# Strassen-form layer 1 of an MLP kernel: the seven products of a round issued in another order, the helper engines' lists reordered with them

## Chip, cores, metric

One NeuronCore of a Trainium2 chip. The metric is device time in microseconds (us) of one launch. PE is the matmul engine (TensorE), DVE is VectorE, ACT is ScalarE, SP issues the large transfers.

## What is computed

Eight sequences of 256 tokens with 512 features go through an attention block, two gelu MLPs of hidden width 2048, and a small per-sequence expert block with a layer norm. Cut to what matters:

```python
attn_out = softmax((x @ Wq) @ (x @ Wk).T * scale) @ (x @ Wv) @ Wp + bp
cms_out  = gelu(attn_out @ cW1 + cb1) @ cW2 + cb2 + one_hot(codes)
modifier = gelu(concat([attn_out, cms_out]) @ mW1 + mb1) @ mW2 + mb2
x = clip(x + cms_out + modifier, 0, 1)
h = gelu(x @ W_down[e] + b_down[e]) @ W_up[e] + b_up[e]      # e per sequence
out = layernorm(x + h) * ln_w[e] + ln_b[e]
```

## The kernel before

**Split numbers.** Every fp32 operand is kept as a high and a low part (`..._hi` written by ACT, `..._lo` = value minus high part by DVE), and every matmul is three matmuls: low weight by high data, high by high, high by low (`mm3`, lines 214 to 216 of the profile).

**Batches and rounds.** The work runs in two batches of four sequences. In each, `pe_mlp` goes through 26 rounds, `it` = 0 to 25. Chunk `i` of the hidden width (24 chunks of 256: 0 to 7 of the first MLP, 8 to 15 the attention half of the second MLP's input, 16 to 23 its other half) starts in round `it = i` and ends in round `i + 1`. Chunks 0 to 7 and 16 to 23 also have a second layer, eight short steps L0 to L7 in round `i + 2`; chunks 8 to 15 are parked and added in later. So rounds 2 to 9 and 18 to 25 hold layer-2 steps between the products, and rounds 10 to 17 hold none.

**The seven products.** Layer 1 of a chunk is a 2 by 2 block product in Strassen's form: seven products, P1 to P7, six matmuls each. P1, P2, P5, P6 of chunk `it` and P7, P4, P3 of chunk `it - 1` share a round. They accumulate in three PSUM banks: P1, P6, P7, P4 one after another on one bank, P2 on the second, P5 and P3 on the third. Between two products on a bank, ACT or DVE takes the running sum:

- s1 after P1 (P6 waits for it), s2 after P6 (P7 waits), c22 after P7 (P4 waits), c21 after P4 (P1 of chunk `i + 2` waits);
- c11 after P2 (P2 of `i + 2` waits); s5 after P5 (P3 and c22 need it), c12 after P3 (P5 of `i + 2` waits).

c11, c22 and c12 are DVE additions at line 975. s1, s2, s5 and c21 are ACT copies (line 555) for chunks below 16; from chunk 16 on they are DVE additions, lines 955 and 965. The gelu of a sum is ACT's line 631.

**What sets the order.** Nothing is scheduled: each engine runs its own hand-written list, and semaphores tie the lists together. The lists of the MLP are `pe_mlp`, `act_mlp` and `dve_mlp`. A waiting instruction holds all that stands behind it on its engine. In a round DVE does, in this order: low parts of the late weights of chunk `it` (two `w_lo` at line 901), four weight sums of chunk `it + 1` (`s_f`, lines 915 to 920), c11 and c22, low parts of the first weights of `it + 1` (three `w_lo`), then c12, with additions of layer 2 (line 1005), low parts of the hidden values (`hid_lo`) and of the second weight (`w_lo`, 128x1024) between them. In rounds 10 to 14 the inputs of the last eight chunks are made (`t_f` at line 1029, `tc_hi` on ACT, `tc_lo` on DVE), ahead of c12, and in rounds 14 and 15 a 128x2048 addition (line 1048) stands behind c12.

Of the kernel before, what the change touches and what calls it, by code (L numbers as in the profile page):

```python
# [17 lines left out]
def build(nc, x, codes, experts, Wq, Wk, Wv, Wp, bp, cW1, cb1, cW2, cb2, mW1, mb1, mW2, mb2,  # L18
# [43 lines left out]
    with ExitStack() as ctx:  # L62
# [376 lines left out]
        def pe_mlp(pe, b):  # L439

            def l1(i, bank, w, t, start):
                hi, lo = (tc_hi, tc_lo) if phase_of(i) == 2 else (ta_hi, ta_lo)
                which = phase_of(i) // 2
                if i in (0, 1, 2 * NQ, 2 * NQ + 1):
                    pe.wait_ge(t_lo, 14 * b + 7 * which + T_NO[t] + 1)
                for k in range(2):
                    last = mm3(ps[BANKS[i % 2][bank]][:, :], w1_hi[i % 2][:, W_NO[w], k, :],
                               w1_lo[i % 2][:, W_NO[w], k, :], hi[:, T_NO[t], k, :], lo[:, T_NO[t], k, :],
                               start and k == 0, k == 1, skip_group_check=True)
                return last  # L450

            def first(i, which):
                g = quad(b, i)
                if which == 1:
                    pe.wait_ge(w1_l1, 3 * g + 2)
                    if i >= 2:
                        pe.wait_ge(c21_done, g - 1)
                    elif b and i == 0:
                        pe.wait_ge(z_sum, 4 * b + 1)
                    else:  # L460
                        pe.wait_ge(ao_done[0], 2 * b + 1 + i)
                    l1(i, 0, "A11", "B11", True).then_inc(p1_mm, 1)
                elif which == 2:
                    if i >= 2:
                        pe.wait_ge(c11_done, g - 1)
                    elif b and i == 0:
                        pe.wait_ge(z_sum, 4 * b + 2)
                    else:
                        pe.wait_ge(ao_done[1], 2 * b + 1 + i)
                    l1(i, 1, "A12", "B21", True).then_inc(p2_mm, 1)  # L470
                elif which == 5:
                    pe.wait_ge(w1_l1, 3 * g + 3)
                    if i >= 2:
                        pe.wait_ge(c12_done, g - 1)
                    else:
                        pe.wait_ge(ao_done[3 - i], 2 * b + 2)
                    l1(i, 2, "S1", "T1", True).then_inc(p5_mm, 1)
                else:
                    pe.wait_ge(s1_done, g + 1)
                    l1(i, 0, "S2", "T2", False).then_inc(p6_mm, 1)  # L480

            def second(i, which):
                g = quad(b, i)
                if which == 7:
                    pe.wait_ge(w1_l2, 2 * g + 2)
                    pe.wait_ge(s2_done, g + 1)
                    l1(i, 0, "S3", "T3", False).then_inc(p7_mm, 1)
                elif which == 4:
                    pe.wait_ge(c22_done, g + 1)
                    l1(i, 0, "A22", "T4", False).then_inc(p4_mm, 1)  # L490
                else:
                    pe.wait_ge(s5_done, g + 1)
                    l1(i, 2, "S4", "B22", False).then_inc(p3_mm, 1)

            def l2(i, k):
                r = l2_of(b, i)
                reg, slot = phase_of(i) // 2, r % 2
                t, j = divmod(k, KT)
                if k == 0:
                    pe.wait_ge(w2_l, r + 1)  # L500
                    pe.wait_ge(hid_l["11"], r + 1)
                    pe.wait_ge(hid_l["21"], r + 1)
                elif k == KT:
                    pe.wait_ge(hid_l["12"], r + 1)
                    pe.wait_ge(hid_l["22"], r + 1)
                if 8 * (r - RB * b) + k >= 2:
                    pe.wait_ge(evac, 8 * r + k - 1)
                elif b:
                    pe.wait_ge(z_sum, 4 * b + 3 + k)
                else:  # L510
                    pe.wait_ge(ao_done[2 + k], 1)
                for c in range(2):
                    w = slice(j * P, (j + 1) * P)
                    last = mm3(ps[6 + k % 2][:, :], w2_hi[reg][:, slot, c, w], w2_lo[reg][:, slot, c, w],
                               hid_hi[reg][:, slot, c, t, :], hid_lo[reg][:, slot, c, t, :], c == 0, c == 1)
                last.then_inc(l2_mm, 1)

            for which in (1, 2):
                first(0, which)
            for which in (1, 2):  # L520
                first(1, which)
            for which in (5, 6):
                first(0, which)
            second(0, 7)
            for which in (5, 6):
                first(1, which)
            for which in (4, 3):
                second(0, which)
            for it in range(2, QB + 2):
                new, old, dn = it < QB, it - 1 < QB, has_l2(it - 2)  # L530
                for step, which in enumerate((1, 2, 7, 5, 6, 4, 3)):
                    if which in (1, 2, 5, 6):
                        if new:
                            first(it, which)
# [26 lines left out]
        def act_w1_first(act, b, i, part):  # L561
            g = quad(b, i)
            a11, a12, _, _ = raw_blocks(i)
            if part == 0:
                act.wait_ge(w1_in[i % 2], 16 * (g // 2) + 16)
                if i >= 2:
                    act.wait_ge(p6_mm, g - 1)
                else:
                    for e in range(KT):
                        act.wait_ge(pv_mm[e], 2 * b + 1 + i)  # L570
                act_copy(w1_hi[i % 2][:, 0, :, :], a11).then_inc(w1_h1, 1)
                act_copy(w1_hi[i % 2][:, 1, :, :], a12).then_inc(w1_h1, 1)
# [201 lines left out]
        def act_mlp(act, b, tail):  # L774
            cms_t = {10: ("B11", "B21"), 11: ("T1",), 12: ("T2", "T3"), 13: ("B22",), 14: ("T4",)}
            for it in range(QB + 2):
# [9 lines left out]
                    act_s(act, b, 1, 1)  # L786
                if 0 < it < QB - 1:
                    act_w1_first(act, b, it + 1, 0)
                if new and ph != 1 and it != 1:
                    act_gelu(act, b, it, "11")  # L790
                if it == 0:
                    act_gelu(act, b, 1, "11")
                if 0 < it < QB - 1:
                    act_w1_first(act, b, it + 1, 1)
                if old and pph != 1:
                    act_gelu(act, b, it - 1, "22")
                    act_hid(act, b, it - 1, "22")
                if it and new and ph < 2:
                    act_s(act, b, it, 5)
                if old and pph != 1:  # L800
                    act_w2(act, b, it - 1)
                if it and new and ph < 2:
                    act_s(act, b, it, 2)
                if old:
                    if pph == 1:
                        act_c21_copy(act, b, it - 1)
                    else:
                        act_gelu(act, b, it - 1, "21")
                        act_hid(act, b, it - 1, "21")
                for name in cms_t.get(it, ()):  # L810
                    act_t(act, b, 1, name)
                if it == QB and not tail:
# [426 lines left out]
        def dve_mlp(dve, b):  # L1239
            for it in range(QB + 2):  # L1240
# [18 lines left out]
                if it == 0:  # L1259
                    dve_c(dve, b, 0, "11")  # L1260
                    dve_c(dve, b, 1, "11")
                elif new and it > 1:
                    dve_c(dve, b, it, "11")
                late = pph == 1
                if 0 < it < QB - 1 and not late:
                    dve_w1_first(dve, b, it + 1)
                down(1)
                if old:
                    dve_c(dve, b, it - 1, "22")
                if 0 < it < QB - 1 and late:  # L1270
                    dve_w1_first(dve, b, it + 1)
                if old and pph != 1:
                    dve_hid(dve, b, it - 1, "11")
                down(2)
                if new and ph == 2:
                    dve_s_pre(dve, b, it, 5)
                if old and pph != 1:
                    dve_hid(dve, b, it - 1, "22")
                down(3)
                if old and pph != 1:  # L1280
                    dve_w2(dve, b, it - 1)
                if new and ph == 2:
# [281 lines left out]
```

## Time and profile before

| what | value |
|---|---|
| median of 3 runs | 1131.21 us (1131.04, 1131.21, 1133.42) |
| profiled execution, its own time | 1133.84 us |
| its span, first to last instruction | 1132.1 us |
| mean granted TensorE clock | 0.977 |
| PE busy | 1064.7 us (94%) |
| DVE busy | 810.8 us (72%) |
| ACT busy | 501.3 us (44%) |
| PE waits for DVE or ACT inside the MLP rounds | 35.3 us |

The profiled execution's own time is 1.7 us above its span. PE's busy time counts the pipelined ends of matmuls, so a product is best read by the distance between starts. Rounds are found in the timeline by the names: `ta` is the input of chunks 0 to 15, `tc` of chunks 16 to 23, and PE's wait before a product is in brackets behind its first matmul. In this execution round 11 of the first batch starts at 313.60 us, round 15 at 353.46, round 17 at 375.14, round 18 at 388.22; the second batch runs the same rounds 537.98 us later.

### The profile page before, as it was taken

How to read it: one execution, taken by the hardware profiler on the slowest of the kernel's cores; microseconds unless marked ns; L12 is line 12 of the kernel's file. 1: busy time of each engine (PE TensorE's matmuls, PEld its weight loads, DVE VectorE, ACT ScalarE, POOL GpSimd, SP SyncE). 2: the span in 40 equal slices, each digit the busy share in tenths (PEclk: the TensorE clock that was granted, in tenths of full speed). 3: DMA queues.
4: the chain of work that ended last, by engine and by line, in shares of the span. 5: the costliest groups of instructions: out<-in, count | busy, mean ns of one | idle time of the engine just before them, and what ended most of it. 6: DMA issues, size and time to landing. Idle time of an engine off the chain costs nothing. (4 is left out here: it accounts for less than half of the span.)

```text
span 1132.1 us, 13953 instructions
## 1 busy us (share of the span) xinstructions
PE 1064.7 (94%) x4985; PEld 884.5 (78%) x4985; DVE 810.8 (72%) x1413; ACT 501.3 (44%) x881; POOL 6.5 (1%) x11
## 2 busy tenths in 40 slices
PE   8999799999999899999999959999999989999975
PEld 6788588888877688888798848888887768888764
DVE  4434886776678887877555988677667888787767
ACT  4425645444254444334354545454425544433350
POOL 0000000000000000000000000000000000000001
PEclk9999899999999999999999969999999999999988
DMA  6500221120243232305507032312023323231341
GB/s 224 186 1 12 64 75 38 41 71 19 75 141 101 92 132 75 130 20 202 195 28 167 23 130 75 112 39 73 19 76 138 104 88 136 75 131 56 98 126 75
DMA packets 55518, 103.69 MB, mean 92 GB/s; under 512 B 3166, under 2 KB 31898, under 8 KB 51354
## 3 DMA queue, kind: packets, MB, share of 16 engines
q1 hardware_dynamic: 55360, 102.78, 27.1%
q8 instruction: 40, 0.66, 0.2%
q14 instruction: 28, 0.23, 0.1%
q10 hardware_dynamic: 90, 0.02, 0.0%
HBM read 81.82 MB, written 20.97 MB: 91 GB/s over the span
## 5 line engine op out<-in xcount | busy, mean ns | idle before, releaser
L1005 DVE TENSOR_TENSOR acc<-bank,acc 128x512 f32<-128x512 f32 x224 | 154.0, 688 | 85.3 <-PE bank L216 85.1
L631 ACT ACTIVATE sbc<-sbc,bias 128x512 f32<-128x512 f32 x112 | 81.0, 724 | 282.8 <-DVE sbc L975 218.5
L214 PE MATMUL bank<-hid_hi,w_lo 128*128 128x512 f32 x512 | 200.7, 392 | 4.4 <-DVE hid_lo L901 1.7
L214 PE MATMUL bank<-ta_hi,w_lo 128*128 128x512 f32 x448 | 179.6, 401 | 26.3 <-DVE sbc L975 16.5
L215 PE MATMUL bank<-hid_hi,w_hi 128*128 128x512 f32 x512 | 199.7, 390 | 0.0
L216 PE MATMUL bank<-hid_lo,w_hi 128*128 128x512 f32 x512 | 199.6, 390 | 0.0
L216 PE MATMUL bank<-ta_lo,w_hi 128*128 128x512 f32 x448 | 177.7, 397 | 0.0
L215 PE MATMUL bank<-ta_hi,w_hi 128*128 128x512 f32 x448 | 177.5, 396 | 0.0
L214 PEld LDWEIGHTS bank<-ta_hi,w_lo 128*128 128x128 f32 x448 | 86.2, 192 | 50.9 <-DVE sbc L975 18.9
L975 DVE TENSOR_TENSOR sbc<-bank,sbc 128x512 f32<-128x512 f32 x144 | 97.5, 685 | 36.3 <-PE bank L216 34.7
L214 PEld LDWEIGHTS bank<-hid_hi,w_lo 128*128 128x128 f32 x512 | 96.3, 188 | 28.2 <-issue 3.4
L216 PEld LDWEIGHTS bank<-hid_lo,w_hi 128*128 128x128 f32 x512 | 96.4, 188 | 20.0
L215 PEld LDWEIGHTS bank<-hid_hi,w_hi 128*128 128x128 f32 x512 | 96.4, 188 | 19.7
L555 ACT ACTIVATE sbc<-bank 128x512 f32<-128x512 f32 x112 | 65.8, 594 | 90.4 <-PE bank L216 90.4
L901 DVE TENSOR_TENSOR w_lo<-w_raw,w_hi 128x256 fp32r<-128x256 f32 (+1 forms) x176 | 95.0, 562 | 10.7 <-ACT w_hi L555 10.7
L216 PEld LDWEIGHTS bank<-ta_lo,w_hi 128*128 128x128 f32 x448 | 85.8, 191 | 18.4
L215 PEld LDWEIGHTS bank<-ta_hi,w_hi 128*128 128x128 f32 x448 | 86.2, 192 | 17.7
L901 DVE TENSOR_TENSOR hid_lo<-sbc,hid_hi 128x512 fp32r<-128x512 f32 x128 | 87.4, 683 | 11.2 <-ACT hid_hi L555 11.1
L214 PE MATMUL bank<-tc_hi,w_lo 128*128 128x512 f32 x224 | 87.5, 391 | 6.2 <-DVE sbc L965 3.8
L555 ACT ACTIVATE w_hi<-w_raw 128x256 fp32r<-128x256 f32 (+1 forms) x176 | 87.2, 523 | 5.6 <-PE bank L216 5.6
L216 PE MATMUL bank<-tc_lo,w_hi 128*128 128x512 f32 x224 | 87.3, 390 | 0.0
L215 PE MATMUL bank<-tc_hi,w_hi 128*128 128x512 f32 x224 | 87.2, 389 | 0.0
(208 smaller groups left out, 1562.2 us busy)
## 6 DMA issues: line engine op xcount, KB each, us to landing
w_raw<-in_L_cond_mW SPq DMA_DIRECT2D x48, 512.0 KB, 3.7
w_raw<-in_L_cond_cW SPq DMA_DIRECT2D x32, 512.0 KB, 4.5
pre_d<-sbc SPq DMA_DIRECT2D x10, 1024.0 KB, 4.6
sbc<-pre_d SPq DMA_DIRECT2D x10, 1024.0 KB, 7.2
x_raw<-in_x SPq DMA_DIRECT2D x4, 1024.0 KB, 6.1
e_raw<-in_L_cond_W_down SPq DMA_DIRECT2D x8, 512.0 KB, 4.6
e_raw<-in_L_cond_W_up SPq DMA_DIRECT2D x8, 512.0 KB, 6.0
out<-acc SPq DMA_DIRECT2D x16, 256.0 KB, 3.3
```

The lines of the kernel that those rows point to most:

```text
L214: nc.tensor.matmul(dst, w_l, a_h, start=start, stop=False, **kw)
L215: nc.tensor.matmul(dst, w_h, a_h, start=False, stop=False, **kw)
L216: return nc.tensor.matmul(dst, w_h, a_l, start=False, stop=stop, **kw)
L555: return nc.scalar.activation(dst, src, ACT.Copy)
L631: nc.scalar.activation(dst, dst, ACT.Gelu, **kw).then_inc(g_done[key], 1)
L901: sub = lambda dst, a, hi: nc.vector.tensor_tensor(dst, a, hi.bitcast(F32), ALU.subtract)
L975: nc.vector.tensor_tensor(dst, ps[BANKS[i % 2][bank]][:, :], dst, ALU.add).then_inc(done, 1)
L1005: nc.vector.tensor_tensor(dst, bank[:, :], dst, ALU.add).then_inc(evac, 1)
```

## The change

Three lists are written in another order, and two waits are added that the new order needs.

- PE: rounds 2 to 25 take the products as 1, 7, 2, 6, 4, 5, 3 where they took 1, 2, 7, 5, 6, 4, 3. Layer-2 step k still follows the k-th place. P6 now waits for the weights' low parts that P5 waited for. Rounds 0 and 1 keep their own order on PE.
- ACT: the gelu of c22 comes ahead of that of c11; s2 comes ahead of s5, and s5 goes behind c21. The first weights of the next chunk wait for P5 of the chunk two back as well.
- DVE: c22 ahead of c11, in round 1 too, where c22 of chunk 0 moves ahead of the first weights of chunk 2; the additions s2 and c21 of the last chunks come ahead of s5.

```diff
@@ pe_mlp
                 else:
+                    pe.wait_ge(w1_l1, 3 * g + 3)
                     pe.wait_ge(s1_done, g + 1)
                     l1(i, 0, "S2", "T2", False).then_inc(p6_mm, 1)
...
-                for step, which in enumerate((1, 2, 7, 5, 6, 4, 3)):
+                for step, which in enumerate((1, 7, 2, 6, 4, 5, 3)):
@@ act_w1_first
                 if i >= 2:
+                    act.wait_ge(p5_mm, g - 1)
                     act.wait_ge(p6_mm, g - 1)
@@ act_mlp
-                if new and ph != 1 and it != 1:
-                    act_gelu(act, b, it, "11")
                 if it == 0:
+                    act_gelu(act, b, 0, "11")
                     act_gelu(act, b, 1, "11")
+                elif it > 1 and old and pph != 1:
+                    act_gelu(act, b, it - 1, "22")
                 if 0 < it < QB - 1:
                     act_w1_first(act, b, it + 1, 1)
+                if it == 1:
+                    act_gelu(act, b, 0, "22")
+                elif it > 1 and new and ph != 1:
+                    act_gelu(act, b, it, "11")
...
@@ dve_mlp
-                elif new and it > 1:
-                    dve_c(dve, b, it, "11")
+                elif old:
+                    dve_c(dve, b, it - 1, "22")
                 late = pph == 1
                 if 0 < it < QB - 1 and not late:
                     dve_w1_first(dve, b, it + 1)
                 down(1)
-                if old:
-                    dve_c(dve, b, it - 1, "22")
+                if new and it > 1:
+                    dve_c(dve, b, it, "11")
                 if 0 < it < QB - 1 and late:
                     dve_w1_first(dve, b, it + 1)
...
```

PE from P4 of round 11 on (the first matmul of each product, told apart by what it waits for: P4 for c22, P5 for c12, P3 for s5, P1 for c21, P7 for s2, P2 for c11), before:

```order
L214 MATMUL bank<-ta_hi,w_lo_64 128x512 [waits c22_done]
...
L214 MATMUL bank<-ta_hi,w_lo_64 128x512 [waits s5_done]
...
L214 MATMUL bank<-ta_hi,w_lo_64 128x512 [waits c21_done,w1_l1]
...
L214 MATMUL bank<-ta_hi,w_lo_64 128x512 [waits c11_done]
...
L214 MATMUL bank<-ta_hi,w_lo_63 128x512 [waits s2_done,w1_l2]
```

and of the change:

```order
L214 MATMUL bank<-ta_hi,w_lo_64 128x512 [waits c22_done]
...
L214 MATMUL bank<-ta_hi,w_lo_63 128x512 [waits c12_done,w1_l1]
...
L214 MATMUL bank<-ta_hi,w_lo_64 128x512 [waits s5_done]
...
L214 MATMUL bank<-ta_hi,w_lo_64 128x512 [waits c21_done,w1_l1]
...
L214 MATMUL bank<-ta_hi,w_lo_63 128x512 [waits s2_done,w1_l2]
...
L214 MATMUL bank<-ta_hi,w_lo_64 128x512 [waits c11_done]
```

P4 had one product (P3) between itself and the next round's P1; now P5 stands there too, and P7 comes ahead of P2.

ACT in the same round, from the first weights of chunk 12 on (`sbc<-bank` are the copies s5, s2 and c21, told apart by the product they wait for), before:

```order
L555 ACTIVATE w_hi_61<-w_raw 128x256
L555 ACTIVATE w_hi_61<-s_f 128x512 [waits s_step]
L555 ACTIVATE sbc<-bank 128x512 [waits p5_mm,pre_out2]
L555 ACTIVATE sbc<-bank 128x512 [waits p6_mm,pre_out2]
L555 ACTIVATE sbc<-bank 128x512 [waits p4_mm,hid_l21]
L555 ACTIVATE tc_hi<-t_f 128x1024 [waits t_step]
```

and of the change:

```order
L556 ACTIVATE w_hi_61<-w_raw 128x256
L556 ACTIVATE w_hi_61<-s_f 128x512 [waits s_step]
L556 ACTIVATE sbc<-bank 128x512 [waits p6_mm,pre_out2]
L556 ACTIVATE sbc<-bank 128x512 [waits p4_mm,hid_l21]
L556 ACTIVATE sbc<-bank 128x512 [waits p5_mm,pre_out2]
L556 ACTIVATE tc_hi<-t_f 128x1024 [waits t_step]
```

s5 moved from ahead of the other two copies to right before `tc_hi`.

DVE in round 1 of a batch, before (chunk 1's late weights, chunk 2's sums, chunk 2's first weights, c22 of chunk 0):

```order
L901 TENSOR_TENSOR w_lo_64<-s_f,w_hi_62 128x512 [waits w1_h2]
L915 TENSOR_TENSOR s_f<-w_raw 128x256 [waits w1_in0,w1_l2,w1_l1]
L916 TENSOR_TENSOR s_f<-w_raw 128x256
L918 TENSOR_TENSOR s_f<-s_f,w_raw 128x256 [waits s_step]
L920 TENSOR_TENSOR s_f<-w_raw,s_f 128x256 [waits s_step]
L901 TENSOR_TENSOR w_lo_63<-w_raw,w_hi_61 128x256 [waits w1_h1] x2
L901 TENSOR_TENSOR w_lo_63<-s_f,w_hi_61 128x512 [waits w1_h1]
L975 TENSOR_TENSOR sbc<-bank,sbc 128x512 [waits p7_mm,s5_done]
```

and of the change:

```order
L910 TENSOR_TENSOR w_lo_64<-s_f,w_hi_62 128x512 [waits w1_h2]
L924 TENSOR_TENSOR s_f<-w_raw 128x256 [waits w1_in0,w1_l2,w1_l1]
L925 TENSOR_TENSOR s_f<-w_raw 128x256
L927 TENSOR_TENSOR s_f<-s_f,w_raw 128x256 [waits s_step]
L929 TENSOR_TENSOR s_f<-w_raw,s_f 128x256 [waits s_step]
L984 TENSOR_TENSOR sbc<-bank,sbc 128x512 [waits p7_mm,s5_done]
L910 TENSOR_TENSOR w_lo_63<-w_raw,w_hi_61 128x256 [waits w1_h1] x2
L910 TENSOR_TENSOR w_lo_63<-s_f,w_hi_61 128x512 [waits w1_h1]
```

c22 moved ahead of the three `w_lo`.

DVE in round 17, from the first sum of chunk 17 to the one that P1 of chunk 18 waits for (L975 is c11 or c22, L955 s5 or s2, L965 c21), before:

```order
L975 TENSOR_TENSOR sbc<-bank,sbc 128x512 [waits p2_mm,s1_done]
L901 TENSOR_TENSOR w_lo_63<-w_raw,w_hi_61 128x256 [waits w1_h1] x2
L901 TENSOR_TENSOR w_lo_63<-s_f,w_hi_61 128x512 [waits w1_h1]
L975 TENSOR_TENSOR sbc<-bank,sbc 128x512 [waits p7_mm,s5_done]
L901 TENSOR_TENSOR hid_lo_56<-sbc,hid_hi_54 128x512 [waits hid_h11]
L955 TENSOR_TENSOR sbc<-bank,sbc 128x512 [waits p5_mm,c22_done]
L901 TENSOR_TENSOR hid_lo_56<-sbc,hid_hi_54 128x512 [waits hid_h22]
L901 TENSOR_TENSOR w_lo_60<-w_raw,w_hi_58 128x1024 [waits w2_h]
L955 TENSOR_TENSOR sbc<-bank,sbc 128x512 [waits p6_mm,c12_done]
L965 TENSOR_TENSOR sbc<-bank,sbc 128x512 [waits c21_done,p4_mm]
```

and of the change:

```order
L984 TENSOR_TENSOR sbc<-bank,sbc 128x512 [waits p7_mm,s5_done]
L910 TENSOR_TENSOR w_lo_63<-w_raw,w_hi_61 128x256 [waits w1_h1] x2
L910 TENSOR_TENSOR w_lo_63<-s_f,w_hi_61 128x512 [waits w1_h1]
L984 TENSOR_TENSOR sbc<-bank,sbc 128x512 [waits p2_mm,s1_done]
L910 TENSOR_TENSOR hid_lo_56<-sbc,hid_hi_54 128x512 [waits hid_h11]
L964 TENSOR_TENSOR sbc<-bank,sbc 128x512 [waits p6_mm,c12_done]
L910 TENSOR_TENSOR hid_lo_56<-sbc,hid_hi_54 128x512 [waits hid_h22]
L910 TENSOR_TENSOR w_lo_60<-w_raw,w_hi_58 128x1024 [waits w2_h]
L974 TENSOR_TENSOR sbc<-bank,sbc 128x512 [waits c21_done,p4_mm]
```

c22 and c11 changed places around the three `w_lo`, and c21 now comes right behind the 128x1024 `w_lo`.

## Rows read from the trace of the kernel before

**Rows 1.** Page, busy time: us, share of the span, instructions of each engine.

```profile
PE 1064.7 (94%) x4985; PEld 884.5 (78%) x4985; DVE 810.8 (72%) x1413; ACT 501.3 (44%) x881; POOL 6.5 (1%) x11
```

**Rows 2.** Table by stretch: us, busy time (instructions) by engine, PEclk, DMA share, GB/s.

```profile
157.00:300.00 143.00, 143.00 (x632) 118.41 (x631) 100.34 (x175) 65.02 (x113) 0.00 (x0) 1.00 0.14 45
400.00:530.00 130.00, 130.00 (x577) 107.60 (x576) 103.49 (x171) 50.22 (x82) 0.00 (x0) 1.00 0.24 86
```

**Rows 3.** PE's waits, whole span: who waited for whom, us in total, times, longest.

```profile
PE bank L214 <- DVE sbc L975: 18.9, 12, 6.9
```

**Rows 4.** Timeline, round 1, batch 2: start, us, engine, operation [idle before <-releaser].

```profile
670.96 0.75 DVE L901 TENSOR_TENSOR w_lo<-w_raw,w_hi 128x256 fp32r<-128x256 f32 x2
672.23 0.68 DVE L975 TENSOR_TENSOR sbc<-bank,sbc 128x512 f32<-128x512 f32 x1
672.97 0.79 PE L214 MATMUL bank<-ta_hi,w_lo 128*128 128x512 f32 x1 [6.94 <-DVE sbc L975]
```

**Rows 5.** Timeline, batch 1, round 11: c11 and c22, then P4 and what follows.

```profile
320.68 1.28 DVE L975 TENSOR_TENSOR sbc<-bank,sbc 128x512 f32<-128x512 f32 x2
322.01 0.50 PE L214 MATMUL bank<-ta_hi,w_lo 128*128 128x512 f32 x1 [0.70 <-DVE sbc L975]
323.52 0.39 PE L214 MATMUL bank<-ta_hi,w_lo 128*128 128x512 f32 x1
323.78 0.60 ACT L555 ACTIVATE sbc<-bank 128x512 f32<-128x512 f32 x1 [1.78 <-PE bank L216]
324.28 1.05 ACT L555 ACTIVATE tc_hi<-t_f 128x1024 fp32r<-128x1024 f32 x1
```

**Rows 6.** Timeline of DVE and PE, batch 1, rounds 14 to 16.

```profile
353.94 1.22 DVE L901 TENSOR_TENSOR tc_lo<-t_f,tc_hi 128x1024 fp32r<-128x1024 f32 x1 [2.64 <-ACT tc_hi L555]
355.08 0.68 DVE L975 TENSOR_TENSOR sbc<-bank,sbc 128x512 f32<-128x512 f32 x1
355.68 2.28 DVE L1048 TENSOR_TENSOR acc<-acc,xf 128x2048 f32<-128x2048 f32 x1
357.88 0.41 DVE L901 TENSOR_TENSOR w_lo<-w_raw,w_hi 128x256 fp32r<-128x256 f32 x1
360.46 1.28 DVE L975 TENSOR_TENSOR sbc<-bank,sbc 128x512 f32<-128x512 f32 x2
361.80 0.50 PE L214 MATMUL bank<-ta_hi,w_lo 128*128 128x512 f32 x1 [1.37 <-DVE sbc L975]
```

**Rows 7.** Timeline of DVE, ACT and PE, batch 1, rounds 17 and 18.

```profile
381.95 0.69 DVE L901 TENSOR_TENSOR w_lo<-s_f,w_hi 128x512 fp32r<-128x512 f32 x1 [0.65 <-ACT w_hi L555]
383.28 0.72 ACT L631 ACTIVATE sbc<-sbc,bias 128x512 f32<-128x512 f32 x1 [1.36 <-DVE sbc L975]
385.65 1.22 DVE L901 TENSOR_TENSOR w_lo<-w_raw,w_hi 128x1024 fp32r<-128x1024 f32 x1 [0.26 <-ACT w_hi L555]
388.22 0.47 PE L214 MATMUL bank<-tc_hi,w_lo 128*128 128x512 f32 x1 [1.91 <-DVE sbc L965]
```

**Rows 8.** The table by stretch again, around waits of PE.

```profile
100.00:105.00 5.00, 5.00 (x30) 5.00 (x31) 3.01 (x7) 0.53 (x2) 0.00 (x0) 0.66 0.00 0
118.00:122.00 4.00, 3.97 (x10) 3.12 (x11) 3.97 (x4) 1.60 (x3) 0.00 (x0) 0.57 0.00 0
124.00:129.00 5.00, 2.07 (x9) 1.42 (x9) 3.53 (x4) 3.11 (x6) 0.00 (x0) 1.00 0.15 29
383.00:393.00 10.00, 7.15 (x29) 5.38 (x30) 7.52 (x13) 6.87 (x12) 0.00 (x0) 1.00 0.01 2
926.00:932.00 6.00, 5.33 (x17) 3.96 (x18) 3.95 (x9) 4.56 (x9) 0.00 (x0) 0.72 0.00 1
```

**Rows 9.** Timeline of PE, the first matmul behind three of these waits.

```profile
99.94 0.36 PE L214 MATMUL bank<-pT_hi,vv_lo 128*128 128x256 f32 x1 [1.76 <-DVE pT_lo L901]
118.03 0.50 PE L214 MATMUL bank<-ta_hi,w_lo 128*128 128x512 f32 x1 [2.11 <-DVE w_lo L901]
926.20 0.47 PE L214 MATMUL bank<-tc_hi,w_lo 128*128 128x512 f32 x1 [1.87 <-DVE sbc L965]
```

More of the change, by code:

```diff
@@ L788, in act_mlp @@
                     act_w1_first(act, b, it + 1, 0)
-                if new and ph != 1 and it != 1:
-                    act_gelu(act, b, it, "11")
                 if it == 0:
+                    act_gelu(act, b, 0, "11")
                     act_gelu(act, b, 1, "11")
+                elif it > 1 and old and pph != 1:
+                    act_gelu(act, b, it - 1, "22")
                 if 0 < it < QB - 1:
                     act_w1_first(act, b, it + 1, 1)
+                if it == 1:
+                    act_gelu(act, b, 0, "22")
+                elif it > 1 and new and ph != 1:
+                    act_gelu(act, b, it, "11")
                 if old and pph != 1:
-                    act_gelu(act, b, it - 1, "22")
                     act_hid(act, b, it - 1, "22")
[L798 to L801, printed above, removed]
+                if it == 1:
+                    act_s(act, b, 1, 5)
+                    act_w2(act, b, 0)
                 if it and new and ph < 2:
                     act_s(act, b, it, 2)
+                if it > 1 and old and pph != 1:
+                    act_w2(act, b, it - 1)
                 if old:
@@ L809, in act_mlp @@
                         act_hid(act, b, it - 1, "21")
+                if it > 1 and new and ph < 2:
+                    act_s(act, b, it, 5)
                 for name in cms_t.get(it, ()):
@@ L1275, in dve_mlp @@
                 if new and ph == 2:
-                    dve_s_pre(dve, b, it, 5)
+                    dve_s_pre(dve, b, it, 2)
                 if old and pph != 1:
@@ L1281, in dve_mlp @@
                     dve_w2(dve, b, it - 1)
-                if new and ph == 2:
-                    dve_s_pre(dve, b, it, 2)
+                if old and pph == 2:
+                    dve_c21_pre(dve, b, it - 1)
                 if it == QB + 1 and b + 1 < NBAT:
@@ L1288, in dve_mlp @@
                     dve_clip(dve, 2 * b)
-                if old and pph == 2:
-                    dve_c21_pre(dve, b, it - 1)
+                if new and ph == 2:
+                    dve_s_pre(dve, b, it, 5)
                 down(5)
```

## The prediction

> **What bounds the kernel now.** I read the busy times first, then stretches of the MLP rounds, then PE's waits, then the timeline around each wait. PE is busy for 1064.7 of 1132.1 us [rows 1]. In the long stretches with layer-2 steps it has no gap at all: 632 matmuls in 143.00 us, 577 in 130.00, so 0.226 us from start to start and **1.36 us for a product or a layer-2 step** of six matmuls, while DVE is busy for 70 to 80% of it [rows 2]. An order of products can gain nothing there; it can only open a wait. What another order can move are PE's waits, and the largest item, 18.9 us in 12 waits, is for DVE's line 975 [rows 3]. They lie at three places of each batch: round 1, rounds 11 to 17, which hold only seven products and so last 7 x 1.36 = 9.52 us, and round 18. The second batch repeats the first to within 0.1 us from round 11 to round 18.
>
> **Steady rounds with layer 2: nothing.** Each place is 2.72 us long. The shortest hand-over is P7 to P4 through c22, with P2 and P6 between before as after. P1 to P6 through s1 shrinks from three places to two, still over 5 us against the 0.6 to 0.7 us of a copy or an addition. c21 gains a place. DVE's c22 stands right behind the place where P7 now is, so the lists still run in step with PE. Zero, both batches.
>
> **Round 1: a gain.** P4 of chunk 0 waits 6.94 us in the second batch and is released by c22. DVE does c22 at 672.23, P4 starts 0.74 us later at 672.97; right ahead of c22 stand the three `w_lo` from 670.96 to 672.23 [rows 4]. These go behind it, so c22 starts at 670.96 and P4 at 671.70: **1.27 us sooner**. The same list runs in the first batch. What is late next is ACT's chain gelu, hidden value, s5, second weight, s2, gelu of c21 behind c22, and it moves with c22. The slow-clock matmuls behind these waits may go too: PE restarts at half clock in both batches, and a restart 1.27 us sooner leaves between 1.3 us more slow time and 1 us less. I take 1.75 us a batch, bounds 0.9 and 2.4: **-3.5 us** (-1.8 to -4.8).
>
> **Rounds 11 to 17: a loss.** Here DVE is the late one. In round 11 it does c11 at 320.68, c22 0.60 later, and P4 starts at 322.01, 0.73 behind c22's start [rows 5]. In the change c22 takes c11's place: P4 can start at 320.68 + 0.73 = 321.41, 0.60 sooner. But P4 now stands one place earlier in the round and has one product more behind it, 1.36 us. The round ends 1.36 - 0.60 = **0.76 later**. What P5 waited for c12 (0.64 us before, in the same round) is inside this: PE reaches P4 at 313.60 + 4 x 1.36 = 319.04 and waits 2.37 us there.
>
> In rounds 12 to 14 a ring forms. ACT's `tc_hi` stood behind the c21 copy, 0.50 us behind its start at 323.78 [rows 5]; it now stands behind s5, and P5 is one product later than P4. From P4: 1.36 to P5, 1.62 to the s5 copy (322.01 to 323.78, less the 0.15 by which a product behind a wait is longer), 0.50 to `tc_hi`, 1.08 to `tc_lo` (`tc_hi` lasts 1.05), 1.14 to c12, 0.60 to the weights, 2.58 to c22 (353.94, 355.08, 355.68; 357.88 to 360.46 [rows 6]), 0.73 to P4: 9.61 us, 9.64 with the small wait's own cost, against a round of 9.52. So about 0.1 us a round, 0.35 in three.
>
> In round 15 the 128x2048 addition of 2.20 us delays c22; before, P4 waited 1.37 us for it at 361.80 [rows 6]. By the same step as in round 11 it loses 0.76 again, wait 2.3 us, and once more in round 16. Summed from 313.60, with 1.51 us for the first product behind a wait (322.01 to 323.52 [rows 5]), I get these starts of rounds (before in brackets): 12 at 325.65 (324.90), 15 at 354.57 (353.46), 16 at 366.56 (364.69), 17 at 377.81 (375.14). **2.67 us late.**
>
> **Rounds 17 and 18: part of it comes back.** P4 of chunk 16 waited 1.4 us for c22 before, since the third `w_lo` ahead of it stood 0.65 us waiting for ACT, which was at c11's gelu [rows 7]. Now c22 is ahead of the `w_lo`: P1's sum at 377.81 + 1.63 = 379.44, then 0.60 and 2.58 to c22 at 382.62, P4 at 383.36, wait 0.1. But the `w_lo` wait is not gone, it moves behind c22: ACT's gelu of c22 starts at 383.35, the third `w_hi` 0.65 later, DVE's third `w_lo` at 384.66. Then come c11 385.26, `hid_lo` 385.86, s2 386.46, and the gelu of c11, hidden value and second weight of ACT, which let the 128x1024 `w_lo` go at 388.22 instead of 385.65. c21 follows 1.15 later at 389.37, and P1 of round 18, which waits for it, starts at 390.10. Before, 388.22 [rows 7]: **1.88 us late** with a wait of some 2.6 us in place of 1.91. To the end of round 18 I find 1.89. The rounds behind have no gap on PE [rows 2], so nothing is recovered. Two batches: **+3.8 us**, bounds +2.5 and +5.0 (0.3 us a batch for each of the two sums of ACT and DVE steps).
>
> **The clock: a loss.** A wait of PE can take its granted clock to half. Around the wait of 1.76 us at 99.94 it fell (0.66 over 5 us), around 2.11 us at 118.03 it fell (0.57 over 4), and from 124 to 129 it stayed, with PE busy for only 2.07 of 5 us. Around 1.91 us at 388.22 it stayed; around the same wait of the second batch, 1.87 us at 926.20, it fell (0.72 over 6) [rows 7 to 9]. That is 3 of 5. Behind the 1.37 us at 361.80 [rows 6] it stayed full. A fall costs between 0.7 us (926.2: round 18 was that much longer than its twin) and 1.7 us (4 x 0.43); I take 1.3. The change makes four new waits of 2.3 to 2.4 us, in rounds 11 and 15 of both batches, where waits of 0.6 to 1.5 us were: two of four fall, **+2.6 us**, bounds 0 and +6.8. The Trainium skill (TensorE: Matmul & The Clock Gate, "What's actually happening") says that the gate's timing is not tied to the start of the kernel and that the point of a change so varies from run to run; by that rule the same program should give several times, and the two twins at 388.2 and 926.2 agree.
>
> **Sum.** -3.5 + 3.8 + 2.6 = +2.9 us. The profiled execution took 1133.84 us, 1.7 above its span and 2.6 above the median; its twin of the median would have one or two slow stretches fewer. I set the difference on the median of the runs, 1131.2 + 2.9 = **1134.1 us**; against the profiled execution it would be 1136.7.
>
> **Rivals.**
> 1. *The waits move as said, the clock holds.* For it: one of two twins at round 18 held. Then -3.5 + 3.8 = +0.3, 1131.5 us. Chance 0.27. With the clock falling in all four and in round 18 too, +0.3 + 6.8 + 1.3 gives 1139.6; that is the upper end, chance 0.07.
> 2. *Faster: the second product between P4 and P1 takes the wait of round 18 away.* PE waited 1.9 us there for c21 in each batch [rows 7], and c21 is now released one product sooner relative to P1. If DVE's list reached c21 in time, that is if ACT's gelu did not hold the third `w_lo`, P1 would start at its place, 387.5: 2.6 us less than I count in each batch. Then -3.5 + 3.8 - 5.2 = -4.9, 1126.3 us. It decides at a c21 by 386.8; I count 389.37, and the 0.65 us at 381.95 shows the hold. Half of it with a good restart in round 1 gives 1128.5. Chance 0.10.
> 3. *Nothing: DVE's slack takes it all.* If c22 was not the last to come in rounds 11 to 16, only round 1 would change, less than 1128 us. PE's 0.73 us behind c22's start at each of these waits speaks against it. Chance 0.02, inside faster.
>
> **How the numbers follow.** The forecast itself, 1132.5 to 1138, has 0.54; its best part lies near the bound of no change. A measurement of this kernel tells 0.2% (2.3 us) from no change. Above 1133.5: most of the forecast and the high case, **0.55**. Between 1128.9 and 1133.5: rival 1 and the forecast's low end, **0.34**. Below: **0.11**. The range leaves out the high case's end and most of rival 2: **1129.5 to 1139**.
>
> **What would show it.** Right: P4 of chunk 0 some 1.3 us sooner behind DVE's sums; in round 11 one PE wait of about 2.4 us and none at P5; rounds 12 to 14 of 9.6 us; a wait of 2.3 us in round 15 and 1.6 in round 16; round 18 starting with a wait of some 2.6 us for c21; the stretches of [rows 2] still without a gap; a mean clock at or below 0.977. Wrong: gaps in those stretches (a list out of step with PE), round 11 no longer than before, or P1 of round 18 without a wait.

## The result

The changed kernel takes 1136.58 us (median of 15 runs, 1132.17 to 1140.16), the kernel before 1131.82 us in the same comparison (15 runs, 1130.58 to 1133.44). The ratio is 1.0042 with a 95% interval of 1.0029 to 1.0054, so 3.3 to 6.1 us **slower**; the forecast was 1134.1 us with a range of 1129.5 to 1139. The profiled execution took 1139.09 us, its span is 1137.3 us, its mean granted clock 0.976. Where several executions are compared below, each compared kernel has its own runs of the kernel before beside it.

The places that the prediction spoke of, in the profile of the changed kernel. PE's waits over the whole span answer to [rows 3]:

```profile
PE bank L214 <- DVE sbc L984: 17.5, 8, 5.7
PE bank L214 <- ACT sbc L556: 7.9, 2, 4.0
PE bank L214 <- DVE sbc L974: 4.8, 2, 2.4
```

The additions that were line 975 are line 984, those of line 965 are line 974. For c11, c22 and c12 PE waits a little less in total than before, 17.5 us for 18.9, but in 8 waits for 12, so each is longer; for c21 of the last chunks it waits 4.8 us for 3.8 (the two waits of 1.91 and 1.87 us, [rows 7] and [rows 9]).

The table by stretch, answering to [rows 2] and [rows 8]:

```profile
157.00:300.00 143.00, 143.00 (x633) 118.40 (x632) 100.07 (x175) 63.73 (x112) 0.00 (x0) 1.00 0.13 45
320.00:324.00 4.00, 4.00 (x13) 3.11 (x13) 2.71 (x5) 0.60 (x1) 0.00 (x0) 0.63 0.48 152
400.00:530.00 130.00, 129.85 (x574) 107.18 (x573) 104.31 (x172) 49.94 (x82) 0.00 (x0) 1.00 0.24 86
860.00:864.00 4.00, 3.87 (x10) 3.04 (x11) 3.08 (x6) 0.76 (x2) 0.00 (x0) 0.57 0.52 164
903.00:908.00 5.00, 4.72 (x14) 3.77 (x15) 2.09 (x5) 1.25 (x3) 0.00 (x0) 0.67 0.16 55
```

The long rounds are as full as they were: 143.00 us in 143.00, and the 0.15 us that are missing in the stretch from 400 belong to the wait of 0.31 us before L3 at 401.06, which is round 18. The three short stretches are new: the granted clock falls to half behind the wait of round 11 in both batches and behind that of round 15 in the second.

The timeline at the waits themselves, DVE and PE (start, length, operation, idle before and releaser): round 1 of the second batch, with the wait for ACT that lies before it, then rounds 11, 15, 16 and 18 of the first.

```profile
658.53 0.47 PE L214 MATMUL bank<-ta_hi,w_lo 128*128 128x512 f32 x1 [4.02 <-ACT sbc L556]
...
672.62 0.42 DVE L929 TENSOR_TENSOR s_f<-w_raw,s_f 128x256 f32<-128x256 f32 x1
672.97 0.68 DVE L984 TENSOR_TENSOR sbc<-bank,sbc 128x512 f32<-128x512 f32 x1
673.57 0.75 DVE L910 TENSOR_TENSOR w_lo<-w_raw,w_hi 128x256 fp32r<-128x256 f32 x2
673.71 0.79 PE L214 MATMUL bank<-ta_hi,w_lo 128*128 128x512 f32 x1 [5.67 <-DVE sbc L984]
...
319.03 1.28 DVE L984 TENSOR_TENSOR sbc<-bank,sbc 128x512 f32<-128x512 f32 x2
319.77 0.50 PE L214 MATMUL bank<-ta_hi,w_lo 128*128 128x512 f32 x1 [2.21 <-DVE sbc L984]
...
362.44 0.50 PE L214 MATMUL bank<-ta_hi,w_lo 128*128 128x512 f32 x1 [2.14 <-DVE sbc L984]
...
373.66 0.50 PE L214 MATMUL bank<-ta_hi,w_lo 128*128 128x512 f32 x1 [1.40 <-DVE sbc L984]
...
384.69 0.69 DVE L910 TENSOR_TENSOR w_lo<-s_f,w_hi 128x512 fp32r<-128x512 f32 x1 [0.64 <-ACT w_hi L556]
...
389.39 0.68 DVE L974 TENSOR_TENSOR sbc<-bank,sbc 128x512 f32<-128x512 f32 x1
...
390.22 0.47 PE L214 MATMUL bank<-tc_hi,w_lo 128*128 128x512 f32 x1 [2.41 <-DVE sbc L974]
```

In round 1, c22 stands right behind the sums and ahead of the `w_lo`, and PE's wait is 5.67 us for the 6.94 of [rows 4]. The length of that wait is a poor measure, though: it also depends on when PE gets there, and it is between 4.5 and 7.2 us in the kernels below that have the same lists in round 1. What holds still is the time from the wait for ACT ahead of it to P4: 15.18 us here (658.53 to 673.71), 16.49 before, from this line to the 672.97 of [rows 4]:

```profile
656.48 0.50 PE L214 MATMUL bank<-ta_hi,w_lo 128*128 128x512 f32 x1 [3.98 <-ACT sbc L555]
```

In round 11 P4 starts 0.74 us behind c22's start, as before, but waits 2.21 us where P4 waited 0.70 [rows 5]. (Counted from one start to the next, a wait reads 0.16 us longer than in the brackets: 2.37, 2.30, 1.56 and 2.57 us here. The prediction and the tables below count so.)

Between round starts (P1's first matmul), first batch, us:

| from P1 of round ... to ... | before | change | e2_new_mid |
|---|---|---|---|
| 2 to 11 | 173.28 | 173.23 | 173.19 |
| 11 to 12 | 11.30 | 13.68 (half clock) | 12.04 |
| 12 to 15 | 28.56 | 29.07 | 29.30 |
| 15 to 16 | 11.23 | 11.96 | 11.96 |
| 16 to 17 | 10.45 | 11.22 | 11.26 |
| 17 to 18 | 13.08 | 12.34 | 12.34 |
| 18 to 19 | 21.86 | 21.85 | 21.86 |

### The profile page after: what moved, and what is told of

It is laid out like the page before. It is cut to its first block and busy times, and to the rows that moved or that the text cites. A ratio compares the mean times of both kernels' runs of the same rounds, so it can differ in the third digit from the quotient of the medians.

```text
span 1137.3 us, 13993 instructions
## 1 busy us (share of the span) xinstructions
PE 1066.9 (94%) x4985; PEld 884.2 (78%) x4985; DVE 810.7 (71%) x1413; ACT 499.3 (44%) x881; POOL 6.5 (1%) x11
## 5 line engine op out<-in xcount | busy, mean ns | idle before, releaser
L214 PE MATMUL bank<-ta_hi,w_lo 128*128 128x512 f32 x448 | 182.2, 407 | 29.9 <-DVE sbc L984 17.5
L215 PE MATMUL bank<-ta_hi,w_hi 128*128 128x512 f32 x448 | 179.9, 402 | 0.0
```

What stands on the lines that cost most here:

```text
L214: nc.tensor.matmul(dst, w_l, a_h, start=start, stop=False, **kw)
L215: nc.tensor.matmul(dst, w_h, a_h, start=False, stop=False, **kw)
```

## The experiments

The theory that the prediction left (A): in rounds 11 to 17 DVE is late, and the new order asks for c22 one product earlier in the round; each late c22 so costs more, and the longer waits bring the clock down. The first rival (B): the new order costs elsewhere, in the long rounds, in the lists or by the added waits.

### Which rounds: e1_old_mid, e2_new_mid, e3_round1

In all three the order is chosen by round; the two added waits stay.

```diff
+        new_order = lambda it: it < 10 or it >= 18      # e1_old_mid
+        new_order = lambda it: 10 <= it < 18            # e2_new_mid
+        new_order = lambda it: False                    # e3_round1
...
-                for step, which in enumerate((1, 7, 2, 6, 4, 5, 3)):
+                for step, which in enumerate((1, 7, 2, 6, 4, 5, 3) if new_order(it) else (1, 2, 7, 5, 6, 4, 3)):
```

`act_mlp` and `dve_mlp` take their list of before or of the change by the same test. In e2_new_mid round 1 is that of before, in the two others c22 of chunk 0 stands where the change has it.

> The change, but rounds 10 to 17 keep the order of before on PE, ACT and DVE. Theory A (the loss is in rounds 11 to 18, where P4's wait for c22 has one product more behind it): only the gain of round 1 is left, some 1.3 us in the second batch and 0.2 to 1.6 in the first: 1128.5 to 1130.5 us where before is 1131.8; rounds 11 to 18 take in each batch what they took before (96.5 us from P1 of round 11 to P1 of round 19). Theory B (the new order costs in the long rounds with layer 2, or through the added waits): no better than 1134 us.

> The kernel before, but rounds 10 to 17 in the new order, round 1 left as before. Theory A: the whole loss without the gain: 3.8 us for the waits and 2 to 5 us for the clock, 1137.5 to 1140.5 us; PE waits of 2.37, 0.1, 0.1, 2.3, 1.56 us before P4 in rounds 11 and 13 to 16, and 1.9 to 2.6 us before P1 of round 18. Theory B: 1133 us or less.

> The kernel before (with the two added waits), with one step moved: in round 1 DVE does c22 of chunk 0 ahead of the first weights of chunk 2. Theory A: the whole gain, 1128.5 to 1130.5 us, the same as e1_old_mid. A rival, that the gain of round 1 is lost again in a later wait: 1131.8 us, as before.

| kernel | median, us | before, us | ratio (95%) | PE waits in rounds 11, 15, 16, 17, 18 (P4, P1 in 18), us |
|---|---|---|---|---|
| e1_old_mid | 1129.53 | 1132.23 | 0.9974 (0.9965 to 0.9983) | 0.85, 1.54, 0.79, 1.36, 2.06 |
| e2_new_mid | 1139.3 | 1132.23 | 1.0062 (1.0046 to 1.0079) | 2.37, 2.30, 1.56, 0.12, 2.56 |
| e3_round1 | 1128.2 | 1132.23 | 0.9964 (0.9952 to 0.9976) | 0.85, 1.54, 0.80, 1.36, 2.07 |

e3_round1 is a little faster than expected (1128.5 to 1130.5), the other two are where A had them: A holds and B falls. The order in rounds 10 to 17 alone makes the kernel 5.2 to 8.9 us slower, more than the whole change does; the one moved c22 of round 1 gives back 2.7 to 5.4. With the new order in all other rounds (e1_old_mid) the time is that of the moved c22 alone, within what the two intervals leave open, so no effect of the new order shows there. From P1 of round 2 to P1 of round 11 it is 173.0 to 173.4 us in every kernel of this document. The two parts sum to between -0.2 and +6.2 us, around the change's 3.3 to 6.1.

e2_new_mid also shows the waits without the clock, since none of rounds 11 to 17 fell to half in its profiled execution: PE's two waits, rounds 11 and 18,

```profile
320.23 0.50 PE L215 MATMUL bank<-ta_hi,w_lo 128*128 128x512 f32 x1 [2.21 <-DVE sbc L1006]
...
389.32 0.47 PE L215 MATMUL bank<-tc_hi,w_lo 128*128 128x512 f32 x1 [2.40 <-DVE sbc L996]
```

and 76.90 us from P1 of round 11 to P1 of round 18 where before took 74.62: **2.28 us** in the first batch. In the second it is 77.16 us for 74.60, 2.56 more, since P4 of one round of the ring waits 0.44 us there and not 0.1. (DVE stood 0.44 us before the weight sums of that round, at 877.42; what it waited for the profile does not name.) The 2.4 us before P1 of round 18 did bring the clock down in this kernel, in the second batch (22.59 us to round 19 for 21.86).

### The clock: e4_warm

```diff
                     elif old:
+                        if which == 4 and it in (11, 15):
+                            fill(b, it - 1, 9)
                         second(it - 1, which)
...
+            def fill(b, i, n):
+                pe.wait_ge(evac, 8 * (RB * b + NQ))
+                for _ in range(n):
+                    nc.tensor.matmul(ps[6][:, :], w1_hi[i % 2][:, W_NO["A22"], 0, :], ta_hi[:, T_NO["T4"], 0, :],
+                                     start=True, stop=True)
```

> The change, with nine matmuls that nothing reads (into a bank that is free in these rounds) put on PE in front of P4 in rounds 11 and 15, where PE waits 2.3 to 2.4 us; nine take 2.05 us. If part of the loss is the clock that falls behind these waits: no stretch at half clock there, 2.5 to 4 us less than the change, 1132.5 to 1134.5 us, and less spread from run to run. If the clock costs nothing (the next wait hides it): 1136.6 us, as the change.

It took 1134.05 us against 1132.23 (1.0012, 1.0003 to 1.0021): 2.5 us less than the change by the medians, 3.4 by the two ratios (+1.4 for +4.8). The work that counts did not move: P4 of round 11 still starts by c22, now 0.17 us behind the last of the nine, and from P1 of round 11 to P1 of round 18 it is 76.82 and 77.14 us in the two batches, what e2_new_mid takes without a fall.

```profile
318.95 0.50 PE L214 MATMUL bank<-ta_hi,w_lo 128*128 128x512 f32 x1 [0.17 <-DVE sbc L992]
...
310.00:325.00 15.00, 14.83 (x66) 11.93 (x65) 11.50 (x18) 8.70 (x16) 0.00 (x0) 1.00 0.32 105
352.00:367.00 15.00, 14.90 (x66) 12.02 (x65) 11.27 (x16) 6.81 (x14) 0.00 (x0) 1.00 0.11 36
```

The first line is the timeline, the others the table by stretch around rounds 11 and 15: granted clock 1.00 in both, and in the second batch too. The spread shrinks: 12 runs lie within 3.0 us (1132.88 to 1135.84), the change's 15 within 8.0. The change's own runs sort by the clock: the six with a mean granted clock of 0.976 or 0.977 took 1137.49 to 1140.16 us, the four with 0.983 to 0.986 took 1132.17 to 1134.80. So the clock is a part of the loss, and most of the scatter. One fall makes its round 1.6 us longer: round 11 to 12 takes 13.68 and 13.62 us in the change with the fall and 12.04 in e2_new_mid without. In the first batch 0.23 us of it come back in rounds 12 to 14 (29.07 for 29.30), in the second nothing does.

### The ring through ACT: e5_tcfirst, and P5 ahead of P4: e9_p5first

```diff
 # e5_tcfirst, act_mlp
-                if it > 1 and new and ph < 2:
-                    act_s(act, b, it, 5)
                 for name in cms_t.get(it, ()):
                     act_t(act, b, 1, name)
+                if it > 1 and new and ph < 2:
+                    act_s(act, b, it, 5)
 # e9_p5first, pe_mlp (s5 ahead of c21 in act_mlp and dve_mlp too)
-                for step, which in enumerate((1, 7, 2, 6, 4, 5, 3)):
+                for step, which in enumerate((1, 7, 2, 6, 5, 4, 3)):
```

> The change, with one step of ACT moved: in rounds 10 to 14 the copies of the new inputs (tc_hi) come ahead of s5 instead of behind it. Theory A (the ring P5, s5, tc_hi, tc_lo, c12, weights, c22, P4 sets the waits): the ring is 1.36 us shorter, so PE's wait for P4 falls from 2.37 to about 1.0 us in round 11, from 0.1 to 0 in rounds 12 to 14 and from 2.30 to about 0.95 in round 15; the 1.56 of round 16 stays. 3.2 us a batch and most of the slow clock: 1128 to 1130 us. If ACT's order is not in the chain: 1136.6, as the change.

> The change with P5 ahead of P4 again (order 1, 7, 2, 6, 5, 4, 3; ACT's and DVE's lists with s5 ahead of c21). Theory A says that the loss of rounds 11 to 17 is the one product more behind P4, and that c22 ahead of c11 alone is worth 0.6 us: P4's waits are then 1.0 us in round 11, 0 in 12 to 14, 0.9 in round 15 and 0.2 in round 16, and rounds 11 to 17 take 2 to 4 us less than in the change; 1126 to 1129 us. If the loss came from c22's and c11's new places in the lists: waits of 2 us stay, 1134 us or more.

e5_tcfirst: 1126.37 us against 1132.37 (0.9945, 0.9932 to 0.9957). e9_p5first: 1126.51 against 1131.83 (0.9943, 0.9930 to 0.9957). e5_tcfirst is 1.6 us faster than the low end of what was expected, e9_p5first lies inside. PE's timeline, rounds 11, 15, 16, 18 of e5_tcfirst:

```profile
318.23 0.50 PE L214 MATMUL bank<-ta_hi,w_lo 128*128 128x512 f32 x1 [0.85 <-DVE sbc L984]
...
357.40 0.50 PE L214 MATMUL bank<-ta_hi,w_lo 128*128 128x512 f32 x1 [0.80 <-DVE sbc L984]
368.61 0.50 PE L214 MATMUL bank<-ta_hi,w_lo 128*128 128x512 f32 x1 [1.39 <-DVE sbc L984]
385.19 0.47 PE L214 MATMUL bank<-tc_hi,w_lo 128*128 128x512 f32 x1 [2.41 <-DVE sbc L974]
```

and rounds 11, 15 and 18 of e9_p5first:

```profile
320.26 0.50 PE L214 MATMUL bank<-ta_hi,w_lo 128*128 128x512 f32 x1 [0.84 <-DVE sbc L984]
...
359.41 0.50 PE L214 MATMUL bank<-ta_hi,w_lo 128*128 128x512 f32 x1 [0.78 <-DVE sbc L984]
...
385.06 0.76 PE L214 MATMUL bank<-tc_hi,w_lo 128*128 128x512 f32 x1 [3.25 <-DVE sbc L974]
```

Both bring the long waits down, by the two ways that A names. With `tc_hi` ahead of s5 the ring is one product shorter: round 11 waits 1.00 us, rounds 12 to 14 last 9.52, round 15 waits 0.96, and the 1.55 us of round 16, which does not hang on the ring, stays. With P5 ahead of P4 the product more behind P4 is gone and c22's earlier place in DVE's list is left as a gain: 1.00, 0.94 and 0.19 us in rounds 11, 15 and 16. P1 of round 18 waits 3.25 us there, since c21 comes behind s5 on DVE again, and round 17 takes 12.93 us for the change's 12.34. From P1 of round 11 to P1 of round 18 it is 72.6 us in e9_p5first, 73.4 in e5_tcfirst, 74.6 before, 76.9 in the change without falls. The order of the change was not bad as such: **one ACT copy behind the wrong neighbour** was worth 3.5 us a batch. Whether `tc_hi` ahead of the c21 copy would gain in the order of before as well was not run.

### Round 18: e6_c21

```diff
 # act_mlp
-                elif it > 1 and old and pph != 1:
-                    act_gelu(act, b, it - 1, "22")
                 if 0 < it < QB - 1:
                     act_w1_first(act, b, it + 1, 1)
+                if it > 1 and old and pph != 1:
+                    act_gelu(act, b, it - 1, "22")
 # dve_mlp
+                if old and pph == 2:
+                    dve_c21_pre(dve, b, it - 1)
                 if old and pph != 1:
                     dve_w2(dve, b, it - 1)
-                if old and pph == 2:
-                    dve_c21_pre(dve, b, it - 1)
```

The two steps are moved in every round that has them, not in round 17 alone.

> The change, with two steps moved: ACT makes the high part of the next first weights ahead of c22's gelu (it stood behind it), and DVE does c21 ahead of the second weight's low part. Theory A (DVE stands waiting for ACT in round 17 and so comes late to c21): PE's wait before P1 of round 18 falls from 2.57 us to 0.5 or less, rounds 11 to 17 keep their waits; 1131.5 to 1133.5 us. If P1 waited for P4's own end and not for the list: 2.57 us stays and 1136.6.

1130.3 us against 1132.37 (0.9982, 0.9971 to 0.9994), 1.2 us below what was expected. PE in round 18:

```profile
386.55 0.47 PE L214 MATMUL bank<-tc_hi,w_lo 128*128 128x512 f32 x1 [0.18 <-DVE sbc L974]
389.59 0.47 PE L214 MATMUL bank<-hid_hi,w_lo 128*128 128x512 f32 x1 [1.42 <-DVE hid_lo L910]
```

P1's wait is 0.18 us for 2.41, so it was the list that it waited for. A part comes back as another wait: L0 waits 1.42 us for the hidden value's low part (0.65 in the change). From P1 of round 17 to P1 of round 18 it is 10.12 us for 12.34, from there to round 19 22.18 for 21.85: 1.9 us less a batch. Twice 1.9 is 3.8, the medians differ by 6.3. The lowest runs of the two kernels differ by 3.4 us (1128.77 and 1132.17), and in the profiled executions the clock fell behind one of the four waits in rounds 11 and 15 here and behind three of four in the change. So the other 2.5 us may be falls, but no run shows why this kernel should have fewer of them.

### DVE's load: e7_pool_old, e8_pool_new, e12_old_resid, e11_resid with e10_act

```diff
 # e7_pool_old, e8_pool_new
-                if it in (14, 15):
-                    dve_resid(dve, b, it - 14)
 ...
-            nc.vector.tensor_tensor(dst, dst, xf[:, t, :, :], ALU.add).then_inc(resid_done, 1)
+            nc.gpsimd.tensor_tensor(dst, dst, xf[:, t, :, :], ALU.add).then_inc(resid_done, 1)
```

> e3_round1 (order of before, c22 of chunk 0 moved) with the two 128x2048 additions of rounds 14 and 15 taken from DVE to GpSimd, which has nothing to do there. Theory A (DVE is what is late in rounds 15 and 16): PE's waits of 1.54 and 0.79 us before P4 go, 2.5 us a batch, 1122.5 to 1124.5 us. If GpSimd's addition slows DVE while it runs, or PE's next wait takes their place: 1126 to 1128.2.

> The change, with the same two additions on GpSimd. Theory A: the waits of 2.30 and 1.56 us in rounds 15 and 16 fall to 0.1, that of 2.37 in round 11 and 2.57 in round 18 stay: 1127 to 1130 us; still 3 us or more above e7_pool_old. If the new order is as good as the old once DVE has room: within 1 us of e7_pool_old.

Both expectations missed, and far: 1142.54 us (1.0091, 1.0078 to 1.0104) and 1149.72 us (1.0157, 1.0143 to 1.0171). GpSimd and DVE in e7_pool_old:

```profile
352.91 9.25 POOL L1384 TENSOR_TENSOR acc<-acc,xf 128x2048 f32<-128x2048 f32 x2 [351.35 <-DVE tc_lo L932]
...
353.20 4.60 DVE L932 TENSOR_TENSOR w_lo<-w_raw,w_hi 128x256 fp32r<-128x256 f32 x1
357.73 4.98 DVE L932 TENSOR_TENSOR w_lo<-s_f,w_hi 128x512 fp32r<-128x512 f32 x1
362.80 0.42 DVE L946 TENSOR_TENSOR s_f<-w_raw 128x256 f32<-128x256 f32 x1
```

Two GpSimd additions of 4.6 us each, and beside them two DVE subtractions that last 4.60 and 4.98 us where the first of them took 0.41 [rows 6] and the sums behind them take 0.42 as ever: each stands until a GpSimd addition is over. P4 of round 15 waits 7.8 us in e7_pool_old and 8.6 in e8_pool_new, and the clock falls behind it. The Trainium skill (SBUF — State Buffer, "Who interferes with whom") says that a DVE instruction with two inputs in SBUF contends with a GpSimd instruction that reads SBUF, and calls the ports that they share an exclusive lock; the two rows, 4.60 us for 0.41, agree. These two runs say nothing about the order, then; it was asked again with the additions kept on DVE.

```diff
 # e12_old_resid (on e3_round1), e11_resid (on e10_act = the change with the moves of e5_tcfirst and e6_c21)
-                if it in (14, 15):
-                    dve_resid(dve, b, it - 14)
+                if it == 20:                      # ahead of down(4)
+                    dve_resid(dve, b, 0)
+                if it == 21:                      # ahead of down(0)
+                    dve_resid(dve, b, 1)
```

The moved additions also wait for the layer-2 sums of the rounds before, and the wait of those sums for the additions moves with them (not shown).

> The change with the moved steps of both e5_tcfirst and e6_c21. Theory A: the two gains add: 1126.4 less twice 1.6 us, 1122 to 1124.5 us; waits of 1.0, 0.95 and 1.56 us in rounds 11, 15, 16 and about 0.3 before P1 of round 18. If they overlap: 1126 us.

> e10_act with the two 128x2048 additions moved on DVE from rounds 14 and 15 to rounds 20 and 21, where the layer-2 steps leave DVE time. Theory A: the waits of 0.95 and 1.56 us before P4 in rounds 15 and 16 go and none comes in rounds 20 and 21: 2.5 to 2.8 us a batch, 1116.5 to 1119.5 us.

> e3_round1 (order of before) with the same two additions moved to rounds 20 and 21. Theory A: the waits of 1.54 and 0.79 us in rounds 15 and 16 go, 2.5 us a batch, 1122 to 1124.5 us. With e11_resid it says which order is better once DVE has room: the new one by 4 us or more if its loss was the lists and not the order.

| kernel | median, us | before, us | ratio (95%) | P1 of round 11 to P1 of round 18, first batch, us |
|---|---|---|---|---|
| e12_old_resid | 1126.39 | 1131.83 | 0.9954 (0.9941 to 0.9968) | 71.96 |
| e10_act | 1122.5 | 1131.83 | 0.9916 (0.9902 to 0.9929) | 71.20 |
| e11_resid | 1118.9 | 1131.83 | 0.9885 (0.9870 to 0.9900) | 68.66 |

e10_act and e11_resid came out as expected. What e6_c21 takes out of the waits comes on top of e5_tcfirst: 1.85 us a batch from round 11 to round 19 (93.40 for 95.25). Counted from the change, each kernel against its own runs of the kernel before, the medians do not add (11 and 7 us alone, 14 together), as they would not if both gains contain the same falls of the clock. With the additions out of rounds 14 and 15 the waits of rounds 15 and 16 go, 2.60 us a batch in the old order (71.96 for the 74.56 of e3_round1) and 2.54 in the new. But 1122 to 1124.5 us was expected of e12_old_resid, and a new wait is why it missed: in round 21 the addition stands ahead of a layer-2 addition, and L2 waits for that one. DVE and PE of e12_old_resid:

```profile
449.61 2.28 DVE L1080 TENSOR_TENSOR acc<-acc,xf 128x2048 f32<-128x2048 f32 x1
451.81 0.68 DVE L1036 TENSOR_TENSOR acc<-bank,acc 128x512 f32<-128x512 f32 x1
...
452.55 0.50 PE L215 MATMUL bank<-hid_hi,w_lo 128*128 128x512 f32 x1 [0.80 <-DVE acc L1036]
455.75 0.50 PE L215 MATMUL bank<-hid_hi,w_lo 128*128 128x512 f32 x1 [0.18 <-DVE acc L1036]
```

Round 21 is 1.6 us longer for it; in e11_resid, with the same wait (0.79 us at 450.15), it is 1.1 us longer. **e11_resid, 1.0 to 1.3% under the kernel before, is faster than the kernels before and after**: the new order, with the next first weights ahead of c22's gelu, `tc_hi` ahead of s5, c21 ahead of the second weight, and the large additions where DVE has time. It is also 7.5 us faster than e12_old_resid, but that does not say which order is better: the moves of e5_tcfirst and e6_c21 were never tried in the order of before, nor in that of e9_p5first, and in e12_old_resid P1 of round 18 still waits 2.0 us for c21.

## Why the prediction was right

- *Steady rounds with layer 2: nothing.* Right: 173.0 to 173.4 us from round 2 to round 11 in every kernel. (Between P7 and P4 stood P5 and P6 before, not P2 and P6 as the prediction has it; two products either way, so nothing hangs on it.)
- *Round 1, -3.5 us.* The step was right: from the wait for ACT to P4 of chunk 0 it is 16.49 and 16.44 us in the second batch of the two kernels with c22 in its old place (before and e2_new_mid) and 15.16 to 15.18 us in all the others, 1.3 us less. That the wait itself went from 6.94 to 5.67 us, the same 1.27, is in part luck: e2_new_mid, with round 1 of before, waits 8.46 us, e3_round1 7.17, e6_c21 4.45. The size of the whole term is less certain. e3_round1 has -4.1 us (-5.4 to -2.7). By the traces, from the wait ahead of round 1 (118.03 us and 656.48 us in the kernel before) to P1 of round 2, the two kernels take 22.6 and 21.4 us in the mean of each batch and the twelve others 21.5 and 20.0, which is 2.5 us less for both batches. One kernel's trace differs from the next by up to 1.5 us there. In the first batch the wait of P4 is gone in the profiled change and one of 1.04 us before P1 of round 2 is left, the ACT chain that the prediction named as late next.
- *Rounds 11 to 17.* The mechanism was right at each place: forecast waits of 2.37, 0.1, 2.3 and 1.6 us, measured 2.37, 0.10, 2.30 and 1.56. The start of round 12 was forecast 12.05 us behind that of round 11, and took 12.04 in e2_new_mid.
- *Round 18.* Forecast a wait of some 2.6 us for c21, measured 2.57, with DVE at 384.69 waiting 0.64 us for ACT's `w_hi`.
- *The size of the two together* was low: 1.88 us a batch forecast, 2.28 and 2.56 measured. The term is the ring: 9.64 us a round forecast, 9.77 and 9.87 measured (29.30 and 29.61 us for rounds 12 to 14 of e2_new_mid, where 28.92 were forecast). The steps that the prediction took from different rows left out 0.1 us a round; the further 0.3 us of the second batch it did not have, taking the second batch as the first, and what held DVE up there is not shown. Two batches make +4.8 instead of +3.8, at the upper end of the bounds of 2.5 to 5.0.
- *The clock, +2.6 us.* Right in size: over many runs e4_warm gives 2.5 to 3.4 us for the four waits. A fall costs 1.4 to 1.6 us, not 1.3, so that is some two falls of four; two were forecast. The number of falls was in part luck. It was taken from 3 of 5 waits of 1.8 to 2.2 us in one execution. Over the profiled executions of all kernels 5 of 14 such waits in rounds 11 and 15 brought a fall. In the profiled execution of the change three of four fell, one reason why it is 2.5 us above the median.
- *Sum.* -3.5 + 3.8 + 2.6 = +2.9 forecast. With the measured terms -4.1 + 4.8 + 2.5 (or 3.4) = +3.2 to +4.1, and +4.8 to +5.7 with the 2.5 us that the traces show for round 1 in place of 4.1; measured +4.8 (3.3 to 6.1). The median of 1136.58 us is 2.5 us above the forecast 1134.1; 0.6 of them are the kernel before, which took 1131.82 us in this comparison and not 1131.21.
- *Rival 2* (the second product between P4 and P1 takes the wait of round 18 away) did not come, but e6_c21 shows that its condition was the right one: with c21 in time the wait falls to 0.18 us and the kernel is faster than before.

## What to carry to other kernels

Where one engine's list is late, moving its consumer to an earlier place in the round does not help the consumer; it only puts more work behind the wait. Reckon each hand-over as two numbers, how much sooner the result comes and how many steps more stand behind its wait, and follow every list that the move reorders on the other engines: here the cost lay in an ACT copy that came to stand behind a later product, and moving that copy alone turned +4.8 us into -6.0. Of the 10.8 us between them some 7 are the waits of the two batches. The slow clock has to be priced with the waits: here up to 1.6 us a time behind waits of some 2 us, in some executions and not in others, and nothing behind those of 1.4 us.

## What the runs showed of the hardware

- A wait of PE of some 2 us brings the granted clock to half in some executions and not in others, and between 1.9 and 2.4 us a longer wait did so no more often than a shorter one. In the profiled executions of all kernels it fell (0.67 or less over the 4.5 us behind the wait) behind 5 of 14 waits of 2.14 to 2.21 us before P4 of rounds 11 and 15: 3 of 4 in the change, 0 of 4 in e2_new_mid, which has the same order in these rounds, 1 of 4 in e6_c21, 1 of 2 in e8_pool_new. Before P1 of round 18 it fell behind 3 of 10 waits of 2.37 to 2.41 us and behind 7 of 10 of 1.86 to 1.91 us; behind the wait of 1.76 us at 99.94 us of [rows 9] in 2 of 14 executions; behind 24 waits of 1.37 to 1.42 us never.
- Nine matmuls that nothing reads, put into each of the four waits of rounds 11 and 15, kept the clock at 1.00 there in the profiled execution, and cost no time.
- A 128x2048 fp32 addition takes 4.6 us on GpSimd and 2.28 on DVE, and beside it a DVE subtraction with both inputs in SBUF took 4.60 us for 0.41 and ended when the GpSimd addition did.
